# An adaptive-LayerNorm block with attention and experts: order of the loads, bias masks per step, second LayerNorm per batch, and a third mask on ScalarE

## The reference

```
ga, gb = sign(.) * max(abs(.), 0.25)
h = layernorm(x) * (1 + ca) + sa
x = x + ga * attention(h)          # 16 heads of 8, causal, ALiBi slopes, softmax, W_o
h = layernorm(x) * (1 + cb) + sb
x = x + gb * experts(h)
```

## Time and profile before

| what | before |
|---|---|
| median of 3 runs | 288.43 us |
| the profiled execution | 289.55 us |
| its span | 287.8 us |
| busy: TensorE matmuls / VectorE / ScalarE / GpSimd | 235.3 / 207.1 / 156.5 / 136.4 us |
| mean granted TensorE clock | 0.872 of full |

### The profile page before, as it was taken

One profiled execution on the slowest core, in us unless ns is written; L12 is line 12 of the kernel. 1 busy time (PEld: TensorE's weight loads), 2 busy tenths in 40 slices (PEclk: granted clock), 3 DMA queues, 4 the chain that ended last, 5 costly groups with the idle time before them and its releaser, 6 DMA issues.

```text
span 287.8 us, 5408 instructions
## 1 busy us (share of the span) xinstructions
PE 235.3 (82%) x1799; PEld 159.0 (55%) x1799; DVE 207.1 (72%) x677; ACT 156.5 (54%) x349; POOL 136.4 (47%) x225
## 2 busy tenths in 40 slices
PE   0865956985979979877788687759997999999994
PEld 0454644753656647655565455435453657677774
DVE  1588795874698997798788697994957386536175
ACT  2075745553695966866576555654665743334330
POOL 8520045499565673383253422542764826161330
PEclk9999985555597997999989867995898899999998
DMA  6324574955603505316215100000000000101011
GB/s 157 99 73 164 110 187 127 316 152 144 166 3 87 156 0 141 101 29 157 58 42 158 45 1 2 2 2 0 7 0 2 0 0 2 36 1 39 0 36 36
DMA packets 18098, 20.43 MB, mean 71 GB/s; under 512 B 1560, under 2 KB 15527, under 8 KB 17007
## 3 DMA queue, kind: packets, MB, share of 16 engines
q1 hardware_dynamic: 16870, 19.63, 25.5%
q10 hardware_dynamic: 688, 0.33, 0.4%
q0 software_dynamic: 512, 0.13, 0.2%
HBM read 14.70 MB, written 5.26 MB: 69 GB/s over the span
## 4 chain that ended last, share of the span: by engine, by line
PE 57%; DVE 23%; issue 6%; DMA 6%; ACT 4%; POOL 3%; ACTq 0%; DVEq 0%; POOLq 0%
PE bank L761 10%; PE bank L779 10%; DVE msk L973 7%; PE bank L692 6%; DVE nmax L1002 5%; DMA Qs<-nmT 4%; PE bank L649 3%; PE bank L790 3%; PE bank L671 2%; PE bank L645 2%; PE bank L697 2%; PE bank L847 2%; DMA yt<-in_w_o 2%; PE bank L841 2%; PE bank L666 2%
## 5 line engine op out<-in xcount | busy, mean ns | idle before, releaser
L429 POOL TENSOR_SCALAR_AFFINE_SELECT PT<-PT 128x256 f32<-128x256 f32 (+1 forms) x96 | 47.0, 495 | 66.3 <-ACT PT L482 65.7
L482 ACT ACTIVATE PT<-bank 128x512 f32<-128x512 f32 x96 | 55.7, 594 | 18.5 <-PE bank L671 10.4
L1002 DVE TENSOR_REDUCE nmax<-bank 128x2 f32<-128x512 f32 x64 | 43.8, 684 | 9.8 <-PE bank L649 9.5
L394 POOL TENSOR_TENSOR ex<-eul,lg 128x32 f32<-128x32 f32 x4 | 21.7, 5427 | 25.3 <-DVE lg L1074 25.3
L645 PE MATMUL bank<-mask 128*128 128x256 bf16 x64 | 20.4, 318 | 15.6 <-DVE nmax L1002 11.2
L649 PE MATMUL bank<-Ks,Qs 78*128 78x256 bf16 x128 | 30.3, 325 | 0.0
L574 ACT ACTIVATE U<-bank 128x256 f32<-128x256 f32 x32 | 12.2, 383 | 31.1 <-PE bank L697 31.0
L671 PE MATMUL bank<-Qs,Ks 80*128 80x256 bf16 x128 | 28.7, 311 | 0.0
L488 ACT ACTIVATE msk<-w1a,cand 128x512 bf16<-128x512 f32 x31 | 22.2, 717 | 9.9 <-DVE cand L985 9.9
L488 ACT ACTIVATE msk<-w2a,cand 128x512 bf16<-128x512 f32 x37 | 26.2, 709 | 0.0
L692 PE MATMUL bank<-PT,Vx 128*32 128x256 f32 x256 | 23.7, 447 | 1.2 <-POOL PT L429 1.0
(11 more groups left out here) (183 smaller groups left out, 542.1 us busy)
## 6 DMA issues: line engine op xcount, KB each, us to landing
Qs<-parts SPq DMA_DIRECT2D x7, 576.0 KB
Ks<-parts SPq DMA_DIRECT2D x7, 576.0 KB
parts<-part SPq DMA_DIRECT2D x8, 384.0 KB, 2.8
rows_bc<-rows_out SPq DMA_DIRECT2D x4, 512.0 KB, 5.9
x_all<-in_x SPq DMA_DIRECT2D x8, 128.0 KB, 6.5
parts<-part SPq DMA_DIRECT2D x8, 128.0 KB, 2.8
out<-ob SPq DMA_DIRECT2D x3, 256.0 KB, 2.3
Qs<-parts SPq DMA_DIRECT2D x4, 144.0 KB
```

Of the source, the lines that this page charges most:

```text
L429: gp.affine_select(out=v, in_=v, compare_op=ALU.is_ge, fill=0.0, base=0, pattern=[[0, v.shape[1]], [1, P]], channel_multiplier=-1).then_in ...
L482: act.activation(PT[:, e % 2, j], psE[u % 2][:, :], ACT.Exp).then_inc(q["exp_done"], 1)
L1002: ve.tensor_reduce(nmax[:, b % 2, 1, h:h + 2], bank.rearrange("p (h k) -> p h k", h=2), axis=AX.X, op=ALU.max, negate=True).then_inc(q["ma ...
```

## The change

It has five parts.

1. SyncE's order. Batch 1's parts are written and its stack is loaded without the wait for batch 0's stacks, and batch 2's parts and stack stand ahead of most row loads. Of the rows, the gates alone (512 KB for all batches) are loaded early. The other three rows follow batch by batch behind the stacks of batches 2 to 5.
2. The transposes of the maxima stand behind two `e_unit`s on TensorE, their copy behind the first exponent on ScalarE, and the row DMAs behind the first select on GpSimd, where there are selects in the step.
3. b1's masks are made one per step in steps 8 to 15, b1's magnitudes at step 7, and the products with b1's masks at step 24.
4. The second LayerNorm goes batch by batch: statistics at step 12 + 4b, root and normalisation on GpSimd one step later, product and sum with the rows on VectorE at 14 + 4b, router statistics at 16 + 4b.
5. ScalarE makes the third mask also for the bits of steps 6, 7, 10, 11, ... 30, 31, which are 14.

```diff
-ROWS_STEP, VEC_STEP, SIZE_STEP, BIAS_STEP, WO_STEP = -7, -4, 3, 20, 5
+ROWS_STEP, VEC_STEP, SIZE_STEP, BIAS_STEP, WO_STEP = -7, -4, 7, 20, 5
...
-LN_STAT_AT = {24: 0, 28: 1, 33: 2}
-LN_USE_AT = {26: 0, 30: 1, 35: 2}
-LN_NEXT_AT = {28: 0, 32: 1, 37: 2}
+AT_STAT2, AT_NORM2, AT_H2, AT_STAT3, AT_RSTD3 = AT_Y, AT_Y + 1, AT_Y + 2, AT_Y + 4, AT_Y + 5
...
-B1_STEP, B1_USE = 4, 16
+B1_STEP, B1_USE = 8, 24
...
-    return 0 <= SLOT[n] < E_LAG
+    return 0 <= SLOT[n] < E_LAG or (SLOT[n] >= E_LAG and SLOT[n] % G >= 2)
...
+            def rows_to_dram():
 
                 sp.wait_ge(q["dve_set"], SETS["rows"])
                 sp.dma_start(rows_dram, rows[:, :, :]).then_inc(q["rows_out"], 16)
...
+            def gate_rows():
                 sp.wait_ge(q["rows_out"], 16)
-                for i in range(ROW_DMAS):
-                    bs = slice(i * B // ROW_DMAS, (i + 1) * B // ROW_DMAS)
-                    sp.dma_start(rows_bc[:, bs].rearrange("p b r d -> p (b r d)"),
-                                 rows_dram[bs].rearrange("b r d -> (b r d)").partition_broadcast(P)).then_inc(rows_in[i], 16)
-
-            def stack(b):
-
+                sp.dma_start(rows_bc[:, :, 0, :], rows_dram[:, 0, :].partition_broadcast(P)).then_inc(q["gate_in"], 16)
+
+            def other_rows(i):
+                bs = slice(i * B // ROW_DMAS, (i + 1) * B // ROW_DMAS)
+                for b in range(bs.start, bs.stop):
+                    sp.dma_start(rows_bc[:, b, 1:4, :], rows_dram[b, 1:4, :].partition_broadcast(P)).then_inc(rows_in[i], 16)
+
...
+            write_parts(0)
+            stack(0)
+            rows_to_dram()
+            write_parts(1)
+            fixed_rows(1)
+            block_in(3)
+            stack(1)
+            block_in(4)
+            gate_rows()
+            bias_rows()
+            fixed_rows(2)
+            write_parts(2)
+            stack(2)
+            block_in(5)
+            other_rows(0)
+            fixed_rows(3)
+            write_parts(3)
+            stack(3)
+            block_in(6)
+            block_in(7)
+            other_rows(1)
+            for b in range(4, B):
+                write_parts(b)
+                stack(b)
+                if b < 6:
+                    other_rows(b - 2)
...
-                gp.wait_ge(rows_in[b * ROW_DMAS // B], 16)
+                gp.wait_ge(q["gate_in"], 16)
...
+            def second_normal(b):
+
+                deviation("ln2_stat", b, ve1, mv1, rs1, "ln2_rstd")
+                gp.wait_ge(q["ln2_rstd"], b + 1)
+                if b >= 2:
+                    gp.wait_ge(q["h2_done"], b - 1)
+                for i in range(NBLK):
+                    k = NBLK * b + i
+                    last = gp.tensor_scalar(n2[:, NBLK * (b % 2) + i, :], x_all[:, b, i, :], mv1[:, k, 0:1], rs1[:, k:k + 1],
+                                            op0=ALU.subtract, op1=ALU.mult)
+                last.then_inc(q["n2_done"], 1)
+
+            def router_ln(b):
+                deviation("ln3_stat", b, ve3, mv3, rs3, "ln3_rstd")
...
-                for k in (2 * i, 2 * i + 1):
-                    gp.tensor_scalar(rmask[:, k % 2, k // 2], b1a[:, :], colsa[:, k // 2:k // 2 + 1], None,
-                                     op0=(ALU.is_gt, ALU.is_lt)[k % 2]).then_inc(q["b1m_done"], 1)
+                gp.tensor_scalar(rmask[:, i % 2, i // 2], b1a[:, :], colsa[:, i // 2:i // 2 + 1], None,
+                                 op0=(ALU.is_gt, ALU.is_lt)[i % 2]).then_inc(q["b1m_done"], 1)
...
                                          pattern=[[0, v.shape[1]], [1, P]], channel_multiplier=-1).then_inc(q["sel_done"], 1)
+                        if j == 0 and batch_at(t, AT_NMT) is not None:
+                            mrows(batch_at(t, AT_NMT))
...
-                if 0 <= t - B1_STEP < NC:
+                if 0 <= t - B1_STEP < 2 * NC:
                     bias_masks(t - B1_STEP)
-                if t - 1 in LN_STAT_AT:
-                    second_ln(LN_STAT_AT[t - 1])
-                if t - 1 in LN_NEXT_AT:
-                    router_ln(LN_NEXT_AT[t - 1])
+                b = batch_at(t, AT_NORM2)
+                if b is not None:
+                    second_normal(b)
+                b = batch_at(t, AT_RSTD3)
+                if b is not None:
+                    router_ln(b)
...
-            second_ln(NPAIR - 1)
-            router_ln(NPAIR - 1)
+            second_normal(B - 1)
+            router_ln(B - 2)
+            router_ln(B - 1)
...
                 exp_unit(t, 0)
+                b = batch_at(t, AT_NMT)
+                if b is not None:
+                    act.wait_ge(q["nmT_done"], b + 1)
+                    if b >= 2:
+                        act.wait_ge(mrow_in[b % 2], 32 * (b // 2))
+                    act.activation(nmT[:, b % 2, :], psO[0:3 * NH, 0:S], ACT.Copy).then_inc(q["nmr_done"], 1)
...
                 s_unit(t, 0)
+                e_unit(t, 0)
+                e_unit(t, 1)
                 b = batch_at(t, AT_NMT)
                 if b is not None:
                     pe.wait_ge(q["nm_split"], b + 1)
...
                     last.then_inc(q["nmT_done"], 1)
-                e_unit(t, 0)
-                e_unit(t, 1)
                 s_unit(t, 1)
...
+            def second_use(b):
+
+                v.wait_ge(q["n2_done"], b + 1)
+                v.wait_ge(rows_in[b * ROW_DMAS // B], 32)
+                dst = h2[:, b // 2, NBLK * (b % 2):NBLK * (b % 2 + 1), :]
+                for r, src in ((2, n2[:, NBLK * (b % 2):NBLK * (b % 2 + 1), :]), (3, dst)):
+                    last = ve.tensor_tensor(dst, src, rows_bc[:, b, r, :].unsqueeze(1).broadcast_to([P, NBLK, D]),
+                                            op=ALU.mult if r == 2 else ALU.add)
                     if r == 2:
                         then_self(last)
                 last.then_inc(q["h2_done"], 1)
...
-                for steps, work in ((LN_NEXT_AT, router_stats), (LN_STAT_AT, second_stats), (LN_USE_AT, second_use)):
-                    if t in steps:
-                        work(steps[t])
-            second_stats(NPAIR - 1)
-            second_use(NPAIR - 1)
-            router_stats(NPAIR - 1)
+                for at, work in ((AT_STAT2, second_stats), (AT_H2, second_use), (AT_STAT3, router_stats)):
+                    b = batch_at(t, at)
+                    if b is not None:
+                        work(b)
+            second_use(B - 1)
+            router_stats(B - 1)
```

99 lines of the change are left out of this document (31 added, 68 removed).

## The result

The changed kernel takes 278.3 us (median of four runs, 277.2 to 281.6), the kernel before 289.1 beside it: ratio 0.961, 95% interval 0.953 to 0.969. The change wins 10.9 us. The forecast was 268.5, a gain of 20. The sign was right, the time lies at the upper edge of the range (262 to 278; the kernel before was itself 0.7 us slower here than the 288.4 that the forecast started from), and half of the expected gain is missing.

What follows compares the result with a forecast made beforehand. In steps 12 to 31 VectorE's work plus waits was taken as the time, in steps 4 to 7 waits at half clock. Terms summed to -20.1 on 289.55, 269.4, put at 268.5 us for the median; range 262 to 278.

Steps and rivals of the forecast that it cites:

- The loads, taken at -9.0: Steps 0 to 11: reordered loads, fewer masks and a higher clock save 9.0 us, bounds 4 to 10.5.
- The waits of 2.21 and 2.92 us: TensorE's waits ahead of the first score tiles of batches 1 and 2; the earlier stack loads were to end them.
- Steps 12 to 23, taken at +1.4, -1.2 and -1.3: Three four-step windows, VectorE's busy time plus waits: first 1.4 us longer, next 1.2 and 1.3 us shorter.
- The third rival: GpSimd's new work slows VectorE, 0.3 us for each of 16 new normalizations, 4.8 in all: 273.3 us; 10%.
- Steps 24 to 31, taken at -8.0: Two windows with the pair's LayerNorm work gone from VectorE: -3.7 us in steps 24 to 27, -4.3 in 28 to 31.
- less than 6 as a sign of being wrong: The prediction is wrong if steps 24 to 31 are not at least 6 us shorter.
- Steps 32 to 40, taken at -2.0: Some half-clock time goes, as the pair's use at step 30 is gone: 2.0 us less, range 0 to 5.
- The row transfers: Maxima's rows issued 2 to 3 us sooner, landing at the same distance, ending TensorE's four waits of 5.2 us.
- the first rival: Maxima's rows stay late, landing when the stack load ends; steps 20 to 27 keep some 6 us: 274.5 us; 15%.
- VectorE's 190 us: Sign over the whole program: VectorE busy about 190 us.
- late selects in steps 13 to 16 alone: Sign: TensorE waits for late selects only in steps 13 to 16; P·V waiting for them elsewhere means wrong.
- the clock back at full before 70 us: Sign in the opening: TensorE's clock at full before 70 us; at half past 75 us means wrong.

Runs made afterwards that it cites:

- the second execution: The changed kernel run again unedited, on another chip, and profiled: 279.7 us.
- a6: Changed kernel with SyncE's order of loads put back as before, masks, second LayerNorm and third mask kept: slower by 9.0 us by the medians, 4.9 by the lowest times.
- a3: Changed kernel with the second LayerNorm back in pairs of batches on VectorE: 282.0 us.
- a11: Changed kernel with b1's masks in steps 24 to 31 and the second LayerNorm in pairs on VectorE: 279.0 us.
- a15: Kernel with b1's masks in steps 4 to 11, with the second LayerNorm back in pairs on VectorE: 278.8 us for 275.7.
- a5: Changed kernel with b1's eight masks one per step in steps 4 to 11 instead of 8 to 15: 275.7 us.
- a7: Changed kernel with GpSimd's second normalization adding the negated mean instead of subtracting the mean: 281.2 us beside 279.7.
- a12: Kernel with b1's masks in steps 4 to 11 (275.7 us), with GpSimd's second normalization two steps later and its followers one to three: 284.0 us.
- a14: Kernel with b1's masks in steps 4 to 11, with the maxima's transposes, copy and row issue back where they stood before: 285.4 us for 275.7.

## Why the prediction was right, and where it was off

**The loads, taken at -9.0: right.** Steps 0 to 11 lost 11.7 us, 8.9 in the second execution. a6 puts the order of the loads at 8.4 there. The clock, of which I took up to 3.3 as part of the gain, was at full from the start in one execution and came back to full only in steps 8 to 11 of the other, and is worth up to 2.8. The waits of 2.21 and 2.92 us are gone: TensorE has no wait over half a microsecond at a batch's first score tile. "Step 12 begun by 83 us" held, at 80.7.

**Steps 12 to 23, taken at +1.4, -1.2 and -1.3: this is the step that failed.** Together they were to be 1.1 us shorter and were 10.1 longer (6.0 in the second execution). The sum was busy time of VectorE plus waits, and it fell short in both. That the time still lies at the edge of the range owes something to luck: the opening gave 2.7 us more than its term, and steps 24 to 31 ran at a full clock (below).

Part of the 10.1 is the clock, for which the sum had no term here: its mean was 0.81, for 0.94 before. The second execution lost 6.0 at 0.86, and a6, which differs by the loads alone, lost 6.8 at 0.92 (67.52 us, VectorE busy 57.7 of them, waits 9.8). So 6 to 7 us of the loss come without a lower clock, most of them as busy time of VectorE (57.7 for 52.3 before).

VectorE's busy time was to be 18.2 + 17.5 + 17.7 = 53.4 us and was 56.9. Its part for the third mask is right: the counts of W2 fell from 7.4 to 3.0 us. What was missing is that its other instructions take longer beside GpSimd. The two products with the rows (0.49 and 0.43 us before) take 0.58 and 0.60 over the whole program, and in steps 12 to 23 the three batches' took 4.8 us where I had 2.7; the small steps of the search (`cand`, `nxt`) took 4.8 for 3.5. These are the two groups over the whole program:

```profile
L1067 DVE TENSOR_TENSOR h<-h,rows_bc 128x256 f32<-128x256 f32 x8 | 4.8, 596 | 0.3
L1067 DVE TENSOR_TENSOR h<-n,rows_bc 128x256 f32<-128x256 f32 x8 | 4.6, 577 | 4.6 <-POOL n L415 4.6
```

The third rival, which I priced at 4.8 us and held at 10%, had the effect right and its cause wrong: it charged the hold-up to the 16 new normalizations. The timelines of VectorE and GpSimd side by side show it elsewhere. Here are two products of VectorE beside GpSimd's split of the parts, and below them one beside GpSimd's root (L405):

```profile
145.00 0.84 DVE L1067 TENSOR_TENSOR h<-n,rows_bc 128x256 f32<-128x256 f32 x1
145.65 1.21 POOL L389 TENSOR_TENSOR part<-resid,part 128x512 bf16<-128x512 f32 x1
145.88 1.26 DVE L1067 TENSOR_TENSOR h<-h,rows_bc 128x256 f32<-128x256 f32 x1
...
196.54 0.75 POOL L405 TENSOR_TENSOR rs<-ve,mhalf 128x2 f32<-128x2 f32 x1
196.75 0.42 DVE L1067 TENSOR_TENSOR h<-h,rows_bc 128x256 f32<-128x256 f32 x1
```

The second product, 0.42 us when nothing is in its way, took 1.26 and ended 0.28 us after the subtraction of GpSimd that had begun 0.23 us before it. Beside the root the same product kept its 0.42. Of the instructions that the changed kernel's trace shows longer than usual by over 0.09 us, all stand beside selects, the split, a mask, the first LayerNorm or the gated W_o, work that GpSimd had before the change as well, and none beside a new normalization. Added up against each instruction's usual time, the hold-up in steps 12 to 23 is 4.3 us (3.7 in the second execution) where it was 0.4 before. In a3, a11 and a15, which have no second LayerNorm in these steps on either engine, it is still 1.9 to 2.6 us, so about half of it is not that LayerNorm's. The Trainium skill (SBUF — State Buffer, SBUF: two separate sides) states that a VectorE instruction with two SBUF inputs and a GpSimd instruction that reads SBUF exclude each other, and that the one which starts first keeps the other out for the whole of its length. The trace agrees for the selects and the split, and not for the root, beside which the product was not held. The maxima's reduction, which reads PSUM, stayed at 0.68 us.

VectorE's waits were to be 6.2 us in these three windows (2.6, 2.0, 1.6) and were 14.0 (10.6 in the second execution). I let the old waits of 3.25 and 3.7 fall and gave GpSimd's lateness 1.2. In fact GpSimd carried 49.3 us of work in 70.9, for 30.0 in 60.7 before. VectorE waited 5.5 us for totals (1.9 before), 4.7 for score tiles (2.7 before), both made by TensorE, which itself stood 3.7 us for selects, and 1.2 for the new n. The masks are some 4 us of the whole, by a5's median; with masks and LayerNorm both away, a11 has the first window back at 18.8 us. The cost of crowding is no sum of GpSimd's microseconds, though: a7 takes 5.5 us of its work away and wins nothing, and a12 more than halves the select waits and wins nothing in these steps. I read this as several limits close together, GpSimd's order, VectorE's longer work and the clock; that is argued from these runs, not shown by one.

**Steps 24 to 31, taken at -8.0: right in the first execution, in part by its clock.** 35.1 us for 43.95, 8.8 less; "steps 28 to 31 in 17 us" came out at 15.5. But the clock stood at 1.00 there, for 0.85 before. In the second execution, at about 0.88, steps 24 to 31 took 39.05 us: 4.9 less, where the prediction had named less than 6 as a sign of being wrong. Undoing the LayerNorm per batch lengthens steps 24 to 30 by 3.1 us at like clocks (a3) and by 11.2 where the clock falls too (a15), so the lumps of a pair's LayerNorm are a cause, as named. What I did not see is that most of this is moved into steps 12 to 23 rather than won (2.6 and 8.0 us), where the forecast had it covered.

**Steps 32 to 40, taken at -2.0: about right.** From the first maximum of step 31 to the end 91.6 us for 93.9, in both executions; from step 32's transposes on 88.8 for 91.05. The clock was full from 187 to 219 us (1.00, where the window of the earlier trace rows had 0.83).

**The row transfers: the right part for another reason.** I gave the maxima's new place an issue 2 to 3 us sooner, and with it the end of TensorE's waits for the rows. They did not land sooner by as much: they took 6.5 us for 4.1 in the median, behind broadcasts and stacks, and TensorE's waits for them fell only from 5.2 to 3.3 us (the first rival, in part). With the same loads but the issue back behind three selects (a14) the median was 3.1 us, for 6.0 in a5: what was issued sooner landed later after its issue. The Trainium skill (DMA: Bandwidth & Descriptors, Queues, rings and completion order) states that a DMA engine takes turns between its queues packet by packet. What I drew from it, that the landing keeps its distance to the issue, does not hold in these traces; the page itself doesn't say it, and no run here shows the turns. Yet the part is worth 7 to 10 us (a14). The one row that changed by as much is ScalarE's wait at the copy, which had stood in front of its counts: 16.2 us of waits became 1.7. That this wait is the cause is likely and not shown, since a14 moves the transposes and the issue as well. The wait stood in the trace before, and I had not read it.

So the parts are worth more than the whole. Undone one at a time (the maxima's place in a5, the others in the changed kernel), the loads cost 5 to 9 us, the maxima's place 7 to 10, the third mask 6 to 8, the LayerNorm 2 to 4: 20 to 31 us, for a gain of 10.9 with the masks' place against it (4). A likely reading, not tested: the middle of the program was loaded with work from its end, and the third mask and the maxima's place pay for that; without either, the same work costs its full price.

Of the signs named, VectorE's 190 us (197.9), no wait over 0.5 for the rows (2.2), and late selects in steps 13 to 16 alone (others of 0.5 to 1.3 us stand at 76, 82, 166, 184 and 199 us) failed. The last is one of the three by which the prediction called itself wrong. ScalarE's 168 (165.5), the clock back at full before 70 us and step 12 held.
